# Null attention: the probabilities are divided by their sums on GpSimd, round by round, instead of the output being scaled by spread inverse sums

## Time and profile before

| what | value |
|---|---|
| time, median of 3 runs | 2984.89 us (2981.12 to 2985.41) |
| time of the profiled execution | 2986.86 us |
| span of the profiled execution | 2985.1 us |
| first scores of the null attention | 1477.33 us from the start |
| one middle batch | 74.99 us |
| first scores of its last batch | 1990.52 us |

### The profile page before, as it was taken

One profiled execution on the slowest core, in us unless ns is written; L12 is line 12 of the kernel. 1 busy time (PEld: TensorE's weight loads), 2 busy tenths in 40 slices (PEclk: granted clock), 3 DMA queues, 4 the chain that ended last, 5 costly groups with the idle time before them and its releaser, 6 DMA issues. The chain is left out here.

```text
span 2985.1 us, 39248 instructions
## 1 busy us (share of the span) xinstructions
PE 2450.5 (82%) x15064; PEld 1672.4 (56%) x15064; DVE 1213.5 (41%) x2325; ACT 1049.7 (35%) x2908; POOL 268.3 (9%) x323
## 2 busy tenths in 40 slices
PE   2464888789997589889899999997998997884894
PEld 2231556556665344444666666665786666664673
DVE  4234666577776221222333333334543444222003
ACT  1311556467775112221233333334321443322211
POOL 0000000000000123223000000002001000002003
PEclk9686999999999799999999999999999999887897
DMA  1100000000000200000200000000001000003332
GB/s 52 51 15 2 1 1 1 29 19 22 12 22 1 85 0 0 0 0 2 105 8 8 8 8 8 1 1 26 1 1 54 29 15 15 1 1 110 117 110 60
DMA packets 51018, 74.71 MB, mean 25 GB/s; under 512 B 8210, under 2 KB 40612, under 8 KB 49444
## 3 DMA queue, kind: packets, MB, share of 16 engines
q1 hardware_dynamic: 49316, 68.20, 6.7%
q0 software_dynamic: 1536, 4.20, 0.5%
HBM read 63.90 MB, written 8.39 MB: 24 GB/s over the span
## 5 line engine op out<-in xcount | busy, mean ns | idle before, releaser
L806 ACT ACTIVATE ca_prob<-bank,ca_nmax 128x512 f32<-128x512 f32 x256 | 174.2, 691 | 93.6 <-DVE ca_nmax L872 93.6
L872 DVE TENSOR_REDUCE ca_nmax<-bank 128x1 f32<-128x512 f32 x256 | 164.0, 682 | 57.0 <-PE bank L664 56.9
L1416 DVE TENSOR_TENSOR rf_hh<-rf_rc,rf_r 128x512 f32<-128x512 f32 x96 | 66.4, 692 | 293.1 <-POOL rf_rc L1322 293.1
L806 ACT ACTIVATE na_prob<-bank,na_nmax 128x257 f32<-128x257 f32 x256 | 118.1, 474 | 180.8 <-DVE na_nmax L872 180.8
L1355 PE MATMUL bank<-rf_xg,rf_W 128*128 128x512 f32 x384 | 179.1, 592 | 0.0
L1348 PE MATMUL bank<-rf_hh,rf_W 128*128 128x512 f32 x384 | 179.1, 592 | 0.0
L806 ACT ACTIVATE ra_prob<-bank,ra_nmax 128x256 f32<-128x256 f32 x256 | 118.4, 484 | 104.0 <-DVE ra_nmax L872 104.0
L678 PEld LDWEIGHTS bank<-cst,ca_prob 128*128 128x128 f32 x1024 | 112.1, 141 | 73.1 <-issue 63.7
L1322 POOL TENSOR_TENSOR rf_rc<-rf_r,rf_cw 128x512 f32<-128x512 f32 x96 | 124.4, 1296 | 286.2 <-ACT rf_r L1377 286.2
L1377 ACT ACTIVATE rf_r<-bank 128x512 f32<-128x512 f32 x96 | 57.3, 597 | 251.7 <-PE bank L1355 251.7
L678 PE MATMUL bank<-cst,ca_prob 128*128 128x128 f32 x1024 | 140.2, 279 | 6.0 <-DVE ca_pT L878 5.2
(11 more groups left out here) (388 smaller groups left out, 4655.6 us busy)
## 6 DMA issues: line engine op xcount, KB each, us to landing
xl_w<-in_L_ffn_w SPq DMA_DIRECT2D x16, 1024.0 KB
rf_W<-in_L_ffn_w SPq DMA_DIRECT2D x2, 3072.0 KB, 14.4
dp_cx<-in_ctx_tok SPq DMA_DIRECT2D x4, 1024.0 KB, 5.5
ca_v<-in_ctx_values SPq DMA_DIRECT2D x8, 512.0 KB, 4.1
na_Wkv<-in_L_xattn_Wkv SPq DMA_DIRECT2D x1, 4096.0 KB
na_cxT<-in_ctx SPq DMA_DIRECT2D x8, 512.0 KB, 3.5
ma_cxT<-in_ctx SPq DMA_DIRECT2D x8, 512.0 KB, 3.5
X<-in_x SPq DMA_DIRECT2D x1, 2048.0 KB
```

The source lines that it names most:

```text
L806: e = act.activation(prob[:, n % 2, u, hh * keys:(hh + 1) * keys], S[u][:, hh * keys:(hh + 1) * keys], ACT.Exp, bias=nmax[:, n % 2, u, hh: ...
L872: v.tensor_reduce(nmax[:, n % 2, u], S[u][:, 0:W].rearrange("p (h k) -> p h k", h=per), AX.X, ALU.max, negate=True).then_inc(maxed, 1)
L1416: v.tensor_tensor(hh[:, c % 3], rc[:, c % 3], r[:, c % 3], ALU.mult).then_inc(hd, 1)
```

```
-    sums = sb("sums", [P, 2, 2, HF])
-    inv = sb("inv", [P, 2, 2, HF])
-    wide = sb("wide", [P, 2, 2, HF, dh])
-    spreadS = sb("spread", [P, 2, 512])
...
-        pnull = sb("pnull", [P, 2, RF, 2, 2])
+        sums = sb("sums", [P, 2, 4])
+        inv = sb("inv", [P, 2, 4])
...
-        if 2 <= n < NR + 2 and (n - 2) % RF == RF - 1:
+        if null is None and 2 <= n < NR + 2 and (n - 2) % RF == RF - 1:
             uses.append(("spread", (n - 2) // RF))
...
                 if null is not None:
-                    po.wait_ge(exped, 4 * n + 4)
-                    po.tensor_copy(pnull[:, f % 2, r2].rearrange("p i a -> p (i a)"), prob[:, n % 2, :, keys - 1])\
-                      .then_inc(null_taken, 1)
-                if r2 == RF - 1:
+                    b, r = divmod(n, R)
+                    po.wait_ge(inverted, n + 1)
+                    for u in range(4):
+                        po.tensor_scalar(prob[:, n % 2, u], prob[:, n % 2, u], inv[:, n % 2, u:u + 1], None, ALU.mult)\
+                          .then_inc(divided, 1)
+                    if r == 0 and b >= 2:
+                        po.wait_ge(ready, ready_at[("null", b - 2)])
+                    po.wait_ge(divided, 4 * n + 4)
+                    po.tensor_copy(pn[:, b % 2, :, 2 * r:2 * r + 2],
+                                   prob[:, n % 2, :, keys - 1].rearrange("p (i a) -> p i a", a=2)).then_inc(null_taken, 1)
+                elif r2 == RF - 1:
...
             def turn(n, f):
...
-                pe.wait_ge(exped, 4 * n + last + 1)
+                pe.wait_ge(exped if null is None else divided, 4 * n + last + 1)
...
-                    pe.wait_ge(null_scaled, FB * (b + 1))
+                    pe.wait_ge(null_taken, R * (b + 1))
...
-                if null is not None:
-                    b, fb = divmod(f, FB)
-                    v.wait_ge(inverted, f + 1)
-                    v.wait_ge(null_taken, RF * (f + 1))
-                    v.tensor_tensor(pn[:, b % 2, :, fb * HF:(fb + 1) * HF].rearrange("p i (r a) -> p i r a", a=2),
...
+            def invert_round(n):
+                v.wait_ge(exped, 4 * n + 4)
+                if n >= 2:
+                    v.wait_ge(divided, 4 * (n - 1))
+                v.reciprocal(inv[:, n % 2], sums[:, n % 2]).then_inc(inverted, 1)
...
-                wait_freed(v, ("spread", f))
-                v.tensor_tensor(outT[:, 2 * fb:2 * fb + 2].rearrange("p m q -> p (m q)"), O[:], spreadS[:, f % 2],
-                                ALU.mult).then_inc(scaled, 1)
+                o = outT[:, 2 * fb:2 * fb + 2].rearrange("p m q -> p (m q)")
+                if null is not None:
+                    v.tensor_copy(o, O[:]).then_inc(scaled, 1)
+                else:
+                    wait_freed(v, ("spread", f))
+                    v.tensor_tensor(o, O[:], spreadS[:, f % 2], ALU.mult).then_inc(scaled, 1)
...
+                if null is not None and n < NR:
+                    invert_round(n)
-                if 1 <= n <= NR and (n - 1) % RF == RF - 1:
+                if null is None and 1 <= n <= NR and (n - 1) % RF == RF - 1:
                     invert((n - 1) // RF)
```

More of the change, by code:

```diff
@@ L530, in attention_stream @@
     pT = sb("pT", [P, 2, GA * NB, 2, P])
-    sums = sb("sums", [P, 2, 2, HF])
-    inv = sb("inv", [P, 2, 2, HF])
-    wide = sb("wide", [P, 2, 2, HF, dh])
-    spreadS = sb("spread", [P, 2, 512])
+    if null is None:
+        sums = sb("sums", [P, 2, 2, HF])
+        inv = sb("inv", [P, 2, 2, HF])
+        wide = sb("wide", [P, 2, 2, HF, dh])
+        spreadS = sb("spread", [P, 2, 512])
     outT = sb("outT", [P, OC, N])
@@ L550, in attention_stream @@
         nvw = sb("nvw", [heads, D])
-        null_taken, null_scaled = g.sem(tag + "_null_taken"), g.sem(tag + "_null_scaled")
+        null_taken, divided = g.sem(tag + "_null_taken"), g.sem(tag + "_divided")
     if reg is not None:
@@ L807, in exps @@
                                        S[u][:, hh * keys:(hh + 1) * keys], ACT.Exp, bias=nmax[:, n % 2, u, hh:hh + 1],
-                                       accum_out=sums[:, f % 2, i, hl:hl + 1])
+                                       accum_out=sums[:, f % 2, i, hl:hl + 1] if null is None
+                                       else sums[:, n % 2, u:u + 1])
                 e.then_inc(exped, 1)
@@ L886, in invert @@
                      .then_inc(inverted, 1)
-                if null is not None:
-                    b, fb = divmod(f, FB)
-                    v.wait_ge(inverted, f + 1)
-                    v.wait_ge(null_taken, RF * (f + 1))
-                    v.tensor_tensor(pn[:, b % 2, :, fb * HF:(fb + 1) * HF].rearrange("p i (r a) -> p i r a", a=2),
-                                    pnull[:, f % 2].rearrange("p r i a -> p i r a"),
-                                    inv[:, f % 2].rearrange("p i (r a) -> p i r a", a=2), ALU.mult)\
-                     .then_inc(null_scaled, 1)
+            def invert_round(n):
[3 more added lines that the diff above has]
+                v.reciprocal(inv[:, n % 2], sums[:, n % 2]).then_inc(inverted, 1)
             def scale(f):
```

## The result

The changed kernel takes **3034.32 us** (median of 4 runs, 3028.05 to 3036.29) against 2983.7 us for the kernel before in the same comparison: ratio **1.0172** [1.0156, 1.0188], 51 us slower. The forecast was slower by 28 us, 3013, with a range of 2978 to 3045: the direction is right, the size is low by 23 us. The time lies outside the forecast's own range (2995 to 3030) and inside the wide one, which took in the two slower rivals. The profiled execution has a span of 3026.2 us (time 3028.05), 41 us over the span before.

What follows compares the result with a forecast made beforehand. TensorE, in order and nearly always busy, bounds the null attention. Loss 8.3 less gain 5.5 is +2.8 us a batch, +17 over six; first batch +8, last +4: +28, 3013 us, range 2978 to 3045.

Steps and rivals of the forecast that it cites:

- the two slower rivals: Null attention: multiply at 1.04 us, 3040 us total, 13%; or TensorE's clock dipping once a batch, 3041 us, 12%.
- The gain: Middle batch of the null attention: four spreads removed from TensorE, 3.92 us, plus waits they caused; 5.5 us a batch.
- the null wait: Round 1: the query product waits in the shared bank until ScalarE empties the null transposes; 0.7 us a batch.
- The stalls: TensorE waiting at the turn for GpSimd's multiplies: 1.03 us in round 1, 1.85 each in 5 and 7, 2.87 in 6.
- Its sum of 8.3: Total loss in a middle batch, us: 1.03 + 0.7 + 1.85 + 2.87 + 1.85.
- X: Price of one 128x257 GpSimd multiply, put at 0.83 us from a tensor_scalar row of the trace.
- the prediction's own rate: One us later start of the turn's second half costs 6 x 4 + 5 + 3 = 32 us of the total.
- T: Earliest start of the turn's second half, after four multiplies: 4.40 us behind the end of VectorE's last product on TensorE.
- The last batch: No products hide the division there: 0.65 us a round for some six rounds, +4 us.
- The first batch: No projection or null step: 12.3 us of stalls less 4.5 for three spreads and waits, +8 us.
- The clock: Rival: TensorE's stalls lower its granted clock, one dip of 3.4 us a batch, 28 in all, 3041 us; 12%.
- round 3: VectorE takes no product, so its reciprocal follows the exponentials: 6.8 us against 7.8 of TensorE work, no stall.

Runs made afterwards that it cites:

- run 2: Changed kernel with each in-place GpSimd multiply replaced by an in-place GpSimd copy of the same 128x257, division left out; 2945.49 us, ratio 0.9891.
- run 7: Changed kernel with extra TensorE products, their results overwritten, ahead of the turn's waits for the division in rounds 5, 6 and 7; 3017.56 us, ratio 1.0132.
- run 8: Changed kernel again, unaltered, profiled a second time in the same comparison as the later runs; 3030.54 us, ratio 1.0164.
- run 4: Changed kernel with the four multiplies moved from GpSimd to VectorE, behind its reciprocal at the late place; 2953.76 us, ratio 0.9913.
- run 3: Changed kernel with VectorE's reciprocal moved ahead of the round's shared products, multiplies unchanged on GpSimd; 2955.25 us, ratio 0.9918.
- run 6: Changed kernel with early reciprocal, null transposes behind the query product, and division split two units each between VectorE and GpSimd; 2940.19 us, ratio 0.9871.
- run 9: Changed kernel with units 0 and 1 multiplied by constant 1.0, singly in even rounds, as one 128x514 instruction in odd; 3020.66 us, single profiled execution.

## Why the prediction was right, and where it was low

**The gain** was put at 5.5 us a batch; the kernel without division gives 5.33, and 0.66 for the null wait that it holds, 6.0. Close, a little low.

**The stalls** stood where the working put them: none behind rounds 0, 2, 3 and 4, the longest behind round 6. In the undisturbed batch of 78.46 us that turn reads:

```profile
1621.06 1.14 PE L674 MATMUL bank<-na_k,na_q 64*128 64x257 f32 x8
1623.94 0.66 PE L688 MATMUL bank<-cst,na_prob 128*128 128x128 f32 x4 [1.74 <-POOL na_prob L640]
1625.76 0.66 PE L688 MATMUL bank<-cst,na_prob 128*128 128x128 f32 x4 [1.17 <-POOL na_prob L640]
```

Without a stall the second half would start 1.535 us after the scores; it starts 4.70 after them, a stall of 3.2 where 2.87 was expected (3.2 with 0.93 us a multiply). Rounds 5 and 7 are alike, 2.1 where 1.85 was expected. The four stalls come to 8.8 us a batch where the working has 7.6. Its sum of 8.3 holds the null wait besides, and with that the runs give 78.45 - 69.00 = 9.45. Gain and loss were both a little low, 0.5 and 1.15, and as the two partly cancel, the undisturbed batch came out close: 78.45 where 77.8 was written.

**X**, the term that the trace before did not show, was read from the right row and 11% low: 0.93 for 0.83. By the prediction's own rate (32 us for one us of T, and T holds four multiplies) that is 32 x 0.4 = 13 us, a little less because one multiply starts under the end of the other (four took 3.66 and not 3.73). The sum with the price corrected, 28 + 13 = 41, compares with the kernel in which the clock hardly falls: 3017.56 against 2981.82, +36.

**The last batch** was put at +4 and came to +8.6, at a clock of 1.00. The dearer multiply gives 3 x 0.4 = 1.2 of the missing 4.6 by the prediction's own rate; what the rest is was not taken apart. The first batch was put at +8 and came to +9.7, with the clock in it.

The Trainium skill's GPSIMD Engine Reference, section 4.1 Engine selection, calls one-input work on GpSimd "roughly line-rate". Measured by VectorE's multiply of the same tile (351 ns), the in-place copy of run 2 agrees (398 ns); this tensor_scalar does not (931 to 933), and the sign of the whole change lay between the two: 2945 at the copy's price, 3034 at the multiply's.

**The clock** was given as a rival with 12%, one dip a batch, 28 us. It came true beside the forecast and not in its place, at about half that size: run 7 against run 8 gives 13 us, and the long middle batches of the two profiles of the changed kernel hold 7.2 and 12.0. This is the step that failed: the cases were treated as exclusive, though stalls up to 3.2 us were part of the forecast itself, and the earlier trace rows showed a fall behind a stretch with 1.3 us of idle time in five. The argument against it, that the stalls stand between dense products, did not hold: the clock fell all the same, though not in every batch. The Trainium skill's TensorE: Matmul & The Clock Gate, in Part 1, says that the array's clock is gated to half when the engine does too little; the rows at 0.70 and 0.62, and a value product of 5.70 for 3.60, agree.

So of the 51 us, about 28 are the forecast's, about 8 to 13 the dearer multiply and the last batch, and about 13 the clock. These come from different comparisons, and a few us of them are the spread between runs.

**Not foreseen at all** was that the place of the reciprocal decides as much as the price. The prediction named the place, behind the shared products, and used it only to count from. That the same multiplies at the same price cost nothing in a middle batch when the reciprocal stands ahead of the shared products was in its own numbers: for round 3, where VectorE takes no product, it found 6.8 us against 7.8 and no stall.

## What to carry to other kernels

When an in-order engine hands work on, look at where in its list the hand-over stands as well as at the price of what is handed over. Here either was enough: at the late place a cheaper instruction (runs 2 and 4), or at the same price an earlier place (run 3), each took some 75 to 90 us off the changed kernel, the clock's share among them. At the early place nothing of the price was left in a middle batch; in the last batch it still counted. Division on VectorE alone at the early place was not run. A rival that can come true together with the forecast is a term of the sum, not a case beside it. And a stall on TensorE in a dense stretch should be priced twice, once for the wait and once for a slower clock behind it.

## What the runs showed of the hardware

- GpSimd's float tensor_scalar in place takes 857 ns for 128x257 with a constant factor, 931 with a factor from a tile, 2.52 ns for each further element; its copy of the same tile takes 398, and VectorE does the same multiply in 351 on average, four of them one behind the other in 1.14 us. Reading the factor from a tile is 74 ns of that.
- Side by side, VectorE and GpSimd slow each other: with two multiplies each, started 0.06 us apart, VectorE's second took 0.57 us instead of 0.35 and GpSimd's first 1.09 instead of 0.93 (run 6).
- The granted clock was 0.70 and 0.62 in two stretches of five us, the first of which holds a stall of 1.74 us. The transposes right behind that stall took 1.05 us instead of 0.66, and the weight loads of the value product after them came 0.85 us apart instead of 0.43 for a while: the lower of the two levels. It did so in two and three of the six middle batches in two profiles of identical instructions, in all six with a stall of 1.57 in place of 1.74 (run 9), and in none of the six with products in most of the stall (run 7).
